# Normalizing and splitting images in the second stage, half an image per unit

## The chip, the cores and the metric

One core of a Trainium2 chip runs the whole program. Its engines work side by side and meet at semaphores: TensorE (PE) multiplies matrices, VectorE (DVE), ScalarE (ACT) and GpSimd (POOL) do elementwise work, SyncE (SP) issues the DMAs. The time is the device time of one execution in microseconds (us); the median of several runs counts.

## The reference, cut to what matters

The input x has 16 images of 32 channels and 128 x 128 pixels, in f32.

```python
x = x + conv_a(gn(x))     # per-image 3x3 depthwise weights mixed by an attention, then a 1x1 conv
x = x + conv_b(gn(x))
# gn: each channel of each image minus its mean, over its standard deviation
# conv_b: hidden = 1x1 conv 32 -> 192, then a 3x3 depthwise conv; q, k, v = split(hidden)
#         out = irfft2(rfft2(8x8 patches of q) * rfft2(8x8 patches of k))
#         result = w_out @ (v * layernorm_over_channels(out))
```

## The kernel before, in words

**First stage.** The loop over images b from -1 to 15 convolves image b on TensorE (`conv_step`, L530), while image b+1 is centred on ScalarE and image b+2 is loaded and its statistics taken on VectorE. ScalarE evacuates the result x2 (`evacuate`, L731), VectorE takes its statistics (`second_stats`), and from them `shifts` makes scale2 and shift2, the second normalization of that image. SyncE stores x2 to DRAM (`store_x2`). Then the image is normalized in place (`norm`, L746, ScalarE), its f16 value is written to xh (`high`, L757, ScalarE), and what f16 leaves over to xl (`low`, L968, VectorE). `store_xn` (L335) writes both, padded to rows of 130, to the DRAM tensor xn_d, in 8 DMAs of 260 KB.

**Second stage.** There are 32 units u, half an image each; b = u // 2. The buffer xs of a unit holds 66 rows of 130 columns, high and low parts on four groups of 32 partitions. There are three such buffers. For each unit VectorE copies eight windows out of xs (`window`, L1109, r from 0 to 7), TensorE multiplies them into 32 groups (`hidden_group`, L575), and ScalarE copies these out (L817). That is the front of a unit; TensorE interleaves it with the end of the unit before (the "tail"): its v chunks (`v_chunk`, L590, which read xs as well), turns (L603) and projections (L612). Then comes the spectral part: for each of eight octets m TensorE makes q (L650) and k (L662), ScalarE copies q (L859), VectorE multiplies (L1215) and adds (`spectrum`, L1201, L1203), and after octets 2, 4 and 7 come the four inverse transforms (L683), copied out to Y by ScalarE (L872). VectorE then normalizes Y over channels, gates it with v (L1144) and adds the projected result to the residual (`residual`, L1151), which was loaded from x2 in DRAM and is stored to `out`.

**The order of the DMAs.** All are issued by SyncE, in the order of its program, and a wait holds back everything behind it. In the second stage one turn of its loop, for u from 1 on, is before the change:

```python
if u < LAST:
    sp.wait_ge(s_hidden_mm, 32 * u + 1)
    load_xs(u + 1)                # L348: 4 loads of 536 KB, each waited for
store_res(u - 1)                  # L404: waits for the last residual; 4 stores, each waited for
sp.wait_ge(s_inverse_mm, 4 * u + 3)
load_res(u, 0)                    # L395: 2 loads of 256 KB
sp.wait_ge(s_res_in, 64 * u + 32)
load_res(u, 1)                    # 2 more, not waited for
```

The functions that the change touches, and their callers:

Of the kernel before, what the change touches and what calls it, by code (L numbers as in the profile page):

```python
# [24 lines left out]
X_SCALE = 256.0  # L25
# [43 lines left out]
def build(nc, t, out):  # L69
# [4 lines left out]
    NB, C, H, W = x.shape  # L74
# [9 lines left out]
    SUMS = 6  # L84

# [7 lines left out]
    with ctx:  # L93
# [19 lines left out]
        s_xs_in = [semaphore(f"xs_in{s}") for s in range(3)]  # L113
        s_res_in = semaphore("res_in")
        s_out_stored = semaphore("out_stored")
# [4 lines left out]
        s_win_room = semaphore("win_room")  # L120
# [57 lines left out]
        s_xl_ready = semaphore("xl_ready")  # L178

# [55 lines left out]
        def take_tables(name):  # L235
# [13 lines left out]
        tiny = {n: take(c) for n, c in (("v_scale", 1), ("v_shift", 1), ("pixel_stats", 96), ("var_eps", 32), ("rstd", 32))}  # L249
# [22 lines left out]
            ("x2_bias0", 1), ("x2_bias1", 1), ("shift1", 1), ("scale2", 1), ("shift2", 1),  # L272
# [20 lines left out]
        win = [take(1632, f16) for _ in range(3)]  # L293
# [21 lines left out]
        def _(sp):  # L315
# [47 lines left out]
            for b in range(-1, NB + 2):  # L363
# [43 lines left out]

            sp.wait_ge(s_xn_out, 128 * NB)
            load_res(0, 0)
            load_res(0, 1)  # L410
# [14 lines left out]
        def _(pool):  # L425
# [11 lines left out]
            for s in range(3):  # L437
                pool.memset(win[s][:, 16 * WIN:1632].bitcast(f32), 0.0).then_inc(s_win_room, 1)
            pool.wait_ge(s_pool_consts, 2)
            pool.wait_ge(s_pads_zero, 2)  # L440
            pool.wait_ge(s_win_room, 3)
# [25 lines left out]
        def _(pe):  # L467
# [111 lines left out]
            def v_chunk(u, k, jr, groups, between):  # L579
# [6 lines left out]
                for tap in range(9):  # L586
                    dy, dx = tap // 3, tap % 3
                    for s in range(2):
                        row = 8 * (2 * s + jr) + dy
                        mm = pe.matmul(v_banks[chunk % 3][64 * s:64 * s + 64, :], v_w[:, 64 * tap:64 * tap + 64],  # L590
                                       at(xs[u % 3], row * WP + 32 * k + dx, [32 * WP, 2], [WP, 8], [1, 32]),
# [123 lines left out]
        def _(act):  # L715
# [10 lines left out]
            def evacuate(b, k):  # L726
                if k == 0 and b > 2:
                    act.wait_ge(s_xl_ready, 4 * (b - 2))
# [11 lines left out]
            def norm(b, i):  # L740

                if b is not None:
# [3 lines left out]
                    act.activation(piece, piece, ACT.Identity, bias=tiny["shift2"], scale=tiny["scale2"]).then_inc(s_x2n_ready, 1)  # L746
# [533 lines left out]
```

## Time and profile before

| | |
|---|---|
| median of 3 runs | 2265.87 us (2260.75 to 2266.81) |
| the profiled execution | 2273.27 us, its span 2271.2 us |
| TensorE busy | 2145.7 us, 94% |
| VectorE busy | 1741.6 us, 77% |
| ScalarE busy | 1432.6 us, 63% |
| GpSimd busy | 517.1 us, 23% |
| mean granted clock of TensorE | 0.971 of full speed |
| DMA moved | 248.21 MB, 109 GB/s over the span |

Busy time is the time in which an engine executes an instruction; an engine can also be idle because it waits for another, or for a DMA. The granted clock is the share of full speed (2.4 GHz) that the chip lets TensorE have. The profile also shows the convolutions ending at 501 us and the first v chunk of the second stage at 560 us; from there on the units repeat.

### The profile page before, as it was taken

How to read it: one execution, taken by the hardware profiler on the slowest of the kernel's cores; microseconds unless marked ns; L12 is line 12 of the kernel's file. 1: busy time of each engine (PE TensorE's matmuls, PEld its weight loads, DVE VectorE, ACT ScalarE, POOL GpSimd, SP SyncE). 2: the span in 40 equal slices, each digit the busy share in tenths (PEclk: the TensorE clock that was granted, in tenths of full speed). 3: DMA queues.
4: the chain of work that ended last, by engine and by line, in shares of the span. 5: the costliest groups of instructions: out<-in, count | busy, mean ns of one | idle time of the engine just before them, and what ended most of it. 6: DMA issues, size and time to landing. Idle time of an engine off the chain costs nothing.

```text
span 2271.2 us, 101012 instructions
## 1 busy us (share of the span) xinstructions
PE 2145.7 (94%) x45303; PEld 1364.8 (60%) x45303; DVE 1741.6 (77%) x4186; ACT 1432.6 (63%) x2629; POOL 517.1 (23%) x323
## 2 busy tenths in 40 slices
PE   6888888977999999999999999999999999999997
PEld 3333333336666666666666666666666666666664
DVE  4666666645888888888888888788888888878886
ACT  3456655656666666666666666666666666666662
POOL 1000000000332222322222222233322322322222
PEclk9989988888999999999999999999999999999998
DMA  7688888876333333333333333333433333333312
GB/s 144 163 220 224 223 219 219 207 193 157 79 83 84 79 90 86 79 78 79 79 79 81 85 83 79 83 88 79 97 85 82 88 79 88 79 78 79 79 40 57
DMA packets 60386, 248.21 MB, mean 109 GB/s; under 512 B 12393, under 2 KB 12658, under 8 KB 53810
## 3 DMA queue, kind: packets, MB, share of 16 engines
q1 hardware_dynamic: 59954, 241.75, 44.9%
q8 instruction: 357, 5.85, 1.1%
q14 instruction: 75, 0.61, 0.1%
HBM read 139.99 MB, written 101.72 MB: 106 GB/s over the span
## 4 chain that ended last, share of the span: by engine, by line
PE 90%; issue 4%; ACT 2%; DVE 2%; DMA 1%; POOL 0%; SPq 0%; POOLq 0%; ACTq 0%
PE bank L590 24%; PE bank L530 17%; PE bank L575 10%; PE bank L662 10%; PE bank L650 9%; PE bank L603 7%; PE bank L683 6%; PE bank L612 5%; DVE arena L1215 2%; ACT arena L826 1%; ACT arena L731 1%; DMA arena<-tap_rows_in 1%; PE bank L544 0%; ACT arena L817 0%; PE bank L492 0%
## 5 line engine op out<-in xcount | busy, mean ns | idle before, releaser
L459 POOL TENSOR_TENSOR arena<-arena 128x8 f32<-128x8 f32 x256 | 492.8, 1925 | 1238.0 <-DVE arena L1125 1235.5
L590 PE MATMUL bank<-arena 128*64 128x512 f16 x4608 | 690.2, 394 | 0.0
L817 ACT ACTIVATE arena<-bank 100x512 f32<-100x512 f32 x1024 | 581.8, 599 | 110.1 <-PE bank L575 79.4
L575 PEld LDWEIGHTS bank<-arena 128*64 128x64 f16 (+1 forms) x8192 | 328.7, 104 | 232.6 <-issue 22.3
L530 PE MATMUL bank<-arena 32*32 32x508 f32 (+1 forms) x9216 | 384.2, 655 | 51.1 <-issue 36.4
L575 PE MATMUL bank<-arena 128*64 128x128 f16 (+1 forms) x8192 | 389.3, 220 | 18.0 <-DVE arena L1109 11.5
L1215 DVE TENSOR_TENSOR arena<-bank,arena 128x512 f32<-128x512 f32 x512 | 328.9, 684 | 48.2 <-issue 44.9
L826 ACT ACTIVATE arena<-bank,arena 128x256 f32<-128x256 f32 x512 | 261.3, 561 | 114.1 <-PE bank L603 111.2
L859 ACT ACTIVATE arena<-bank 128x512 f32<-128x512 f32 x256 | 152.9, 597 | 225.7 <-PE bank L650 223.9
L1144 DVE TENSOR_TENSOR arena<-arena,bank 128x512 f32<-128x512 f32 x256 | 174.8, 683 | 139.6 <-ACT arena L826 139.6
L650 PE MATMUL bank<-arena 100*32 100x128 f32 x8192 | 276.1, 275 | 1.3 <-ACT arena L817 1.3
L662 PE MATMUL bank<-arena 100*32 100x128 f32 x8192 | 274.8, 274 | 0.2 <-issue 0.2
L1119 DVE BATCH_NORM_STATS2 arena<-arena 128x6 f32<-128x128 f32 x1024 | 221.6, 278 | 65.4 <-ACT arena L872 65.4
L590 PEld LDWEIGHTS bank<-arena 128*64 128x64 f16 x4608 | 206.6, 109 | 95.8 <-issue 11.9
L530 PEld LDWEIGHTS bank<-arena 32*32 32x32 f32 x9216 | 144.7, 107 | 189.6 <-issue 157.6
L872 ACT ACTIVATE arena<-bank 128x256 f32<-128x256 f32 x512 | 155.1, 389 | 147.5 <-PE bank L683 147.5
L662 PEld LDWEIGHTS bank<-arena 100*32 100x32 f32 x8192 | 222.3, 110 | 29.2 <-DVE arena L1215 23.5
L650 PEld LDWEIGHTS bank<-arena 100*32 100x32 f32 x8192 | 217.4, 110 | 19.7 <-ACT arena L817 1.6
L1139 DVE TENSOR_TENSOR arena<-arena 128x512 f32<-128x512 f32 x256 | 177.3, 692 | 37.3 <-POOL arena L459 17.3
L603 PEld LDWEIGHTS bank<-arena 128*128 128x128 f32 x1024 | 133.9, 195 | 107.5 <-issue 68.8
L603 PE MATMUL bank<-arena 128*128 128x128 f32 x1024 | 181.6, 300 | 8.2 <-ACT arena L826 7.1
L683 PE MATMUL bank<-arena 32*64 32x256 f32 x5120 | 171.6, 384 | 15.3 <-DVE arena L1215 12.9
(113 smaller groups left out, 1655.9 us busy)
## 6 DMA issues: line engine op xcount, KB each, us to landing
arena<-xn_d SPq DMA_DIRECT2D x128, 536.2 KB, 4.8
xn_d<-arena SPq DMA_DIRECT2D x130, 260.0 KB, 4.4
x_d<-arena SPq DMA_DIRECT2D x64, 512.0 KB, 8.1
arena<-x_d SPq DMA_DIRECT2D x128, 256.0 KB, 4.1
out<-arena SPq DMA_DIRECT2D x128, 256.0 KB, 2.7
arena<-x_in SPq DMA_DIRECT2D x32, 544.0 KB, 9.6
arena<-x_in SPq DMA_DIRECT2D x32, 528.0 KB, 9.4
arena<-spectra_in SPq DMA_DIRECT2D x1, 384.0 KB
```

The lines of the kernel that those rows point to most:

```text
L459: pool.tensor_tensor(tiny["rstd"][:, slot], tiny["var_eps"][:, slot], powers, ALU.pow).then_inc(s_root, 1)
L530: mm = pe.matmul(at(psum_of(t, r)[32 * c:32 * c + 32, :], low, [W, 4], [1, high - low]), conv_w[b % 2][32 * r:32 * r + 32, 32 * tap:32 * t ...
L575: mm = pe.matmul(ring[g % len(ring)][low:high, 128 * i:128 * i + 128], w[:, first + low:first + high], hidden_w, start=True, stop=True)
L590: mm = pe.matmul(v_banks[chunk % 3][64 * s:64 * s + 64, :], v_w[:, 64 * tap:64 * tap + 64], at(xs[u % 3], row * WP + 32 * k + dx, [32 * WP ...
L603: tr = pe.transpose(t_bank[:, 128 * i:128 * i + 128], at(Y, 8 * k + 4 * jr + i, [32, 128]), ident)
L650: mm = pe.matmul(q_bank[32 * c:32 * c + 32, first:first + 128], G_q[0:WIN, 64 * ch + 32 * part:64 * ch + 32 * part + 32], hwin[0:WIN, 128 ...
L662: mm = pe.matmul(k_banks[m % 2][32 * c:32 * c + 32, first:first + 128], G_k[0:WIN, 64 * ch + 32 * part:64 * ch + 32 * part + 32], hwin[0:W ...
L683: mm = pe.matmul(i_banks(e)[c][64 * lam:64 * lam + 64, 256 * (e % 2):256 * (e % 2) + 256], small["inverse"][32 * c:32 * c + 32, 64 * table ...
L817: act.activation(h_rows[0:WIN, :, first:first + 4], ring[g % len(ring)][0:WIN, :].rearrange("p (i c) -> p c i", i=4), ACT.Copy).then_inc(s ...
L826: ins = act.activation(at(gated[jr], 256 * lam, [32, 8], [8, 4], [1, 8]), at(banks[4], 64 * lam, [8, 8], [128, 4], [1, 8]), ACT.Identity, ...
L1119: ins = dve.bn_stats(T["pixel_stats"][:, first:first + 6], at(Y, 2048 * s + 4 * p + j, [32, 64], [1, 2]))
L1215: dve.tensor_tensor(prod[:, first:first + 512].rearrange("p (a b x) -> p a b x", a=2, b=2), at(k_banks[m % 2], 256 * quad, [128, 2], [0, 2 ...
```

## The change

Only images 0 and 1 (`EARLY = 2`) are still normalized, split and stored to xn_d in the first stage. For the other 14 images the first stage keeps scale2 and shift2 (now one column for each image) and does no `norm`, `high`, `low` or `store_xn`. The second stage does this work instead, in 28 halves: in each of the units 0 to 27, SyncE loads 64 raw rows of x2 (`load_half`), ScalarE does `norm_half` twice and `high_half` twice between the q copies of the spectral part, VectorE `low_half` once after octet 4 and once at the end, and SyncE stores the result with 8 DMAs (`store_half`). The half made in unit u is unit u + 4. Its buffers take the place of the third xs buffer. With two buffers left, the upper 42 rows of the next xs (`load_top`, one DMA at a time) are loaded once the last v chunk of the unit before has been made, and the lower 24 rows (`load_bottom`, two at a time) in the next turn. `load_res` is now called one turn later for the unit that ended, and waits for both of its pairs. The windows of a unit wait for the upper rows at r = 0 and for the lower ones at r = 5.

```diff
+    EARLY = 2
+    TOP = 42
+    HALVES = 2 * (NB - EARLY)
...
-        xs_late = take(HALF * WP, f16)
+        half_x2 = take(2048)
         top[0] = max(top[0], stage1_end)
-        xs = [take(HALF * WP, f16) for _ in range(2)] + [xs_late]
+        xs = [take(HALF * WP, f16) for _ in range(2)]
+        half_high, half_low = [take(16 * WP, f16) for _ in range(2)]
...
-            def load_xs(u, paced=True):
-                b, half = divmod(u, 2)
+            def load_xs(u, landed, first, last, at_once):
+                b, h = divmod(u, 2)
                 for g in range(4):
-                    src = xn_d[b, g % 2, :, half * (H // 2):half * (H // 2) + HALF, :].rearrange("c h w -> c (h w)")
-                    sp.dma_start(xs[u % 3][32 * g:32 * g + 32, :], src).then_inc(s_xs_in[u % 3], 16)
-                    if paced:
-                        sp.wait_ge(s_xs_in[u % 3], 64 * (u // 3) + 16 * (g + 1))
+                    src = xn_d[b, g % 2, :, h * (H // 2) + first:h * (H // 2) + last, :].rearrange("c h w -> c (h w)")
+                    sp.dma_start(xs[u % 2][32 * g:32 * g + 32, first * WP:last * WP], src).then_inc(landed[u % 2], 16)
+                    if (g + 1) % at_once == 0:
+                        sp.wait_ge(landed[u % 2], 64 * (u // 2) + 16 * (g + 1))
+            def load_top(u, at_once):
+                load_xs(u, s_top_in, 0, TOP, at_once)
+            def load_bottom(u, at_once):
+                load_xs(u, s_bottom_in, TOP, HALF, at_once)
...
-                if b == NB + 1:
-                    load_xs(1, paced=False)
-                if older is not None:
+                if older is not None and older < EARLY:
                     sp.wait_ge(s_xl_ready, 4 * (older + 1))
                     store_xn(older)
-                if b == NB - 3:
-                    sp.wait_ge(s_xn_out, 128 * (older + 1))
+                if b in (NB - 3, NB + 1):
+                    u = (b - NB + 3) // 4
+                    sp.wait_ge(s_xn_out, 128)
                     sp.wait_ge(s_pads_stored, 32)
-                    load_xs(0, paced=False)
+                    load_top(u, 8)
+                    load_bottom(u, 8)
...
-            def load_res(u, pair):
-                for s in range(2):
-                    p0 = 64 * pair + 32 * s
-                    sp.dma_start(res[p0:p0 + 32, :].rearrange("p (l r) -> p l r", l=2),
+            def load_res(u):
+                for part in range(4):
+                    pair, s = divmod(part, 2)
+                    sp.dma_start(res[32 * part:32 * part + 32, :].rearrange("p (l r) -> p l r", l=2),
                                  image_rows(x2_d, u // 2, u % 2, pair, s)).then_inc(s_res_in, 16)
+                    if s == 1:
+                        sp.wait_ge(s_res_in, 64 * u + 16 * (part + 1))
...
+            def load_half(u):
+                b, h = divmod(u + 2 * EARLY, 2)
+                if u > 0:
+                    sp.wait_ge(s_half_low, 2 * u)
+                for g in range(4):
+                    first = (64 * h + 16 * g) * W
+                    sp.dma_start(half_x2[32 * g:32 * g + 32, :], x2_d[b, :, first:first + 16 * W]).then_inc(s_half_in, 16)
+                    if g in (1, 3):
+                        sp.wait_ge(s_half_in, 64 * u + 16 * (g + 1))
+            def store_half(u):
+                b, h = divmod(u + 2 * EARLY, 2)
+                done = 128 * EARLY + 128 * u
+                if u == 0:
+                    sp.wait_ge(s_half_pads, 2)
+                sp.wait_ge(s_half_low, 2 * (u + 1))
+                for part, buf in ((0, half_high), (1, half_low)):
+                    for g in range(4):
+                        first = 1 + 64 * h + 16 * g
+                        sp.dma_start(xn_d[b, part, :, first:first + 16, :].rearrange("c h w -> c (h w)"),
+                                     buf[32 * g:32 * g + 32, :]).then_inc(s_xn_out, 16)
+                        if g == 3:
+                            sp.wait_ge(s_xn_out, done + 64 * (part + 1))
+            for s in range(3):
+                sp.wait_ge(s_x2_out[s], 64 * len(range(s, NB, 3)))
+            sp.wait_ge(s_shift2, NB)
+            load_half(0)
             for u in range(1, LAST + 1):
+                sp.wait_ge(s_inverse_mm, 4 * u - 1)
+                if u > 1:
+                    load_bottom(u, 2)
+                load_res(u - 1)
+                if u <= HALVES:
+                    store_half(u - 1)
+                if u < HALVES:
+                    load_half(u)
                 if u < LAST:
-                    sp.wait_ge(s_hidden_mm, 32 * u + 1)
-                    load_xs(u + 1)
+                    sp.wait_ge(s_v_mm, 8 * u)
+                    sp.wait_ge(s_xn_out, 128 * EARLY + 128 * min(u, HALVES))
+                    load_top(u + 1, 1)
                 store_res(u - 1)
-                sp.wait_ge(s_inverse_mm, 4 * u + 3)
-                load_res(u, 0)
-                sp.wait_ge(s_res_in, 64 * u + 32)
-                load_res(u, 1)
+            sp.wait_ge(s_inverse_mm, 4 * LAST + 4)
+            load_res(LAST)
             store_res(LAST)
...
             def norm(b, i):
-                if b is not None:
+                if b is not None and b < EARLY:
                     act.wait_ge(s_shift2, b + 1)
                     act.wait_ge(s_x2_out[b % 3], 64 * (b // 3 + 1))
                     piece = x2[b % 3][:, QPIX // 2 * i:QPIX // 2 * (i + 1)]
-                    act.activation(piece, piece, ACT.Identity, bias=tiny["shift2"], scale=tiny["scale2"]).then_inc(s_x2n_ready, 1)
+                    act.activation(piece, piece, ACT.Identity, bias=tiny["shift2"][:, b:b + 1], scale=tiny["scale2"][:, b:b + 1]).then_inc(s_x2n_ready, 1)
...
+            def norm_half(u, i):
+                if u < HALVES:
+                    b, piece = u // 2 + EARLY, half_x2[:, 1024 * i:1024 * i + 1024]
+                    act.wait_ge(s_shift2, b + 1)
+                    act.wait_ge(s_half_in, 64 * (u + 1))
+                    act.activation(piece, piece, ACT.Identity, bias=tiny["shift2"][:, b:b + 1], scale=tiny["scale2"][:, b:b + 1]).then_inc(
+                        s_half_norm, 1)
+            def high_half(u, i):
+                if u < HALVES:
+                    act.wait_ge(s_half_norm, 2 * u + i + 1)
+                    act.wait_ge(s_xn_out, 128 * EARLY + 128 * u)
+                    act.activation(half_high.rearrange("p (h w) -> p h w", w=WP)[:, 8 * i:8 * i + 8, 1:W + 1],
+                                   half_x2[:, 1024 * i:1024 * i + 1024].rearrange("p (h w) -> p h w", w=W), ACT.Copy).then_inc(s_half_high, 1)
             def spectral(u, tail):
                 for m in range(8):
...
                     act.activation(q_sb[m % 2], q_bank, ACT.Copy).then_inc(s_q_copied, 1)
                     if m == 0 and tail is not None:
                         turned_out(tail, 3, 1)
+                    if m in (1, 4):
+                        norm_half(u, m // 4)
+                    if m in (2, 6):
+                        high_half(u, m // 4)
...
-                    dve.wait_ge(s_xs_in[u % 3], 64 * (u // 3 + 1))
+                    dve.wait_ge(s_top_in[u % 2], 64 * (u // 2 + 1))
+                if r == TOP // 8:
+                    dve.wait_ge(s_bottom_in[u % 2], 64 * (u // 2 + 1))
                 dve.tensor_copy(win[(8 * u + r) % 3][:, 0:16 * WIN].rearrange("p (j y x) -> p j y x", y=10, x=10),
-                                     at(xs[u % 3], 8 * r * WP, [8, 16], [WP, 10], [1, 10])).then_inc(s_win_ready, 1)
+                                     at(xs[u % 2], 8 * r * WP, [8, 16], [WP, 10], [1, 10])).then_inc(s_win_ready, 1)
...
+            def low_half(u, i):
+                if u < HALVES:
+                    dve.wait_ge(s_half_high, 2 * u + i + 1)
+                    padded = lambda a: a.rearrange("p (h w) -> p h w", w=WP)[:, 8 * i:8 * i + 8, 1:W + 1]
+                    dve.tensor_tensor(padded(half_low), half_x2[:, 1024 * i:1024 * i + 1024].rearrange("p (h w) -> p h w", w=W),
+                                      padded(half_high), ALU.subtract).then_inc(s_half_low, 1)
...
+                    if n == 9:
+                        low_half(u, 0)
                 if u < LAST:
                     for r in range(3):
                         window(u + 1, r)
-            dve.wait_ge(s_win_room, 3)
+                low_half(u, 1)
```

## Rows read from the trace of the kernel before

**Rows 1.** Stretches: length, busy PE, PEld, DVE, ACT, POOL; clock; DMA share; GB/s.

```profile
64.46:121.06 56.60, 50.21 (x1177) 21.24 (x1178) 35.07 (x100) 31.07 (x37) 2.19 (x6) 0.91 0.76 192
149.36:478.51 329.15, 286.97 (x6469) 119.55 (x6470) 212.53 (x557) 190.64 (x210) 12.03 (x33) 0.89 0.85 217
478.51:501.10 22.59, 21.57 (x580) 10.31 (x580) 10.77 (x20) 11.69 (x11) 0.70 (x1) 1.00 0.79 190
501.10:534.80 33.70, 14.37 (x264) 11.82 (x263) 14.84 (x26) 27.89 (x42) 0.70 (x1) 0.66 0.81 192
...
613.77:667.49 53.72, 53.11 (x1122) 36.73 (x1124) 44.28 (x104) 35.82 (x72) 15.43 (x8) 1.00 0.36 83
```

**Rows 2.** Waits of PE, 700 to 2188: us in total, times, longest.

```profile
PE bank L683 <- DVE arena L1215: 11.7, 27, 0.8
```

**Rows 3.** Waits of SyncE's queue, 700 to 2188: us in total, times, longest.

```profile
SPq L348 <- DMA arena<-xn_d: 407.3, 81, 7.0
SPq L404 <- DMA out<-arena: 227.0, 84, 4.1
SPq L395 <- DMA arena<-x_d: 106.6, 28, 4.6
```

**Rows 4.** Timeline of SyncE, 1400 to 1462: start, from first issue to last, line.

```profile
1422.82 5.67 SPq L395 DMA_DIRECT2D arena<-x_d  x4
```

**Rows 5.** DMA issues, 700 to 2188: count, size of each, median us to landing.

```profile
arena<-xn_d SPq DMA_DIRECT2D x108, 536.2 KB, 4.8
out<-arena SPq DMA_DIRECT2D x112, 256.0 KB, 2.7
arena<-x_d SPq DMA_DIRECT2D x112, 256.0 KB, 4.1
```

**Rows 6.** DMA issues in the first stage, 120 to 420.

```profile
xn_d<-arena SPq DMA_DIRECT2D x80, 260.0 KB, 4.4
```

**Rows 7.** Timeline of PE, 1400 to 1462: start, us, line.

```profile
1416.99 1.12 PE L683 MATMUL bank<-arena 32*64 32x256 f32 x32
...
1450.41 1.02 PE L612 MATMUL bank<-arena 128*64 128x512 f32 x4
```

**Rows 8.** Timeline of DVE, 1400 to 1462; in brackets the idle time before.

```profile
1413.64 1.29 DVE L1215 TENSOR_TENSOR arena<-bank,arena 128x512 f32<-128x512 f32 x2 [0.53 <-issue]
...
1417.19 1.29 DVE L1215 TENSOR_TENSOR arena<-bank,arena 128x512 f32<-128x512 f32 x2 [0.20 <-issue]
1418.39 1.54 DVE L1109 COPY arena<-arena 128x1600 f16<-128x1600 f16 x3
...
1433.81 0.57 DVE L1109 COPY arena<-arena 128x1600 f16<-128x1600 f16 x1
...
1440.51 0.68 DVE L1151 TENSOR_TENSOR arena<-bank,arena 128x512 f32<-128x512 f32 x1
```

**Rows 9.** Timeline of ACT, 1400 to 1462.

```profile
1455.92 0.60 ACT L859 ACTIVATE arena<-bank 128x512 f32<-128x512 f32 x1 [0.89 <-PE bank L650]
1457.71 0.60 ACT L859 ACTIVATE arena<-bank 128x512 f32<-128x512 f32 x1 [1.20 <-PE bank L650]
```

**Rows 10.** Groups of instructions by shape, 120 to 420: busy, mean ns, idle before.

```profile
L968 DVE TENSOR_TENSOR arena<-arena 128x1024 f16<-128x1024 f32 x40 | 48.8, 1222 | 0.3
...
L738 ACT ACTIVATE arena<-arena 128x1024 f32<-128x1024 f32 x20 | 22.9, 1147 | 0.0
```

**Rows 11.** The chain that ended last, 495 to 562: start, us, what.

```profile
503.60 1.81 ACT arena L757
...
555.20 2.38 issue
```

**Rows 12.** The page's costliest groups, window copies of ScalarE.

```profile
L817 ACT ACTIVATE arena<-bank 100x512 f32<-100x512 f32 x1024 | 581.8, 599 | 110.1 <-PE bank L575 79.4
```

**Rows 13.** Busy time by stretch around a stall of PE.

```profile
154.00:156.00 2.00, 0.00 (x0) 0.00 (x0) 0.83 (x1) 0.55 (x1) 0.00 (x0) 1.00 0.69 240
158.00:170.00 12.00, 12.00 (x183) 3.81 (x151) 3.71 (x13) 2.29 (x2) 0.89 (x2) 0.50 0.71 169
```

More of the change, by code:

```diff
@@ L112, in build @@
         s_transforms_in = semaphore("transforms_in")
-        s_xs_in = [semaphore(f"xs_in{s}") for s in range(3)]
+        s_top_in = [semaphore(f"top_in{s}") for s in range(2)]
+        s_bottom_in = [semaphore(f"bottom_in{s}") for s in range(2)]
         s_res_in = semaphore("res_in")
+        s_half_in = semaphore("half_in")
         s_out_stored = semaphore("out_stored")
@@ L248, in build @@
         powers = take(8)
-        tiny = {n: take(c) for n, c in (("v_scale", 1), ("v_shift", 1), ("pixel_stats", 96), ("var_eps", 32), ("rstd", 32))}
+        tiny = {n: take(c) for n, c in (("v_scale", 1), ("v_shift", 1), ("pixel_stats", 96), ("var_eps", 32), ("rstd", 32), ("scale2", NB), ("shift2", NB))}
         phases = top[0]
@@ L287, in build @@
         res = take(2048)
-        xs_late = take(HALF * WP, f16)
+        half_x2 = take(2048)
         top[0] = max(top[0], stage1_end)
-        xs = [take(HALF * WP, f16) for _ in range(2)] + [xs_late]
+        xs = [take(HALF * WP, f16) for _ in range(2)]
+        half_high, half_low = [take(16 * WP, f16) for _ in range(2)]
         G_q = take(64 * 64)
         G_k = take(64 * 64)
-        win = [take(1632, f16) for _ in range(3)]
+        win = [take(16 * WIN, f16) for _ in range(3)]
         block = ctx.enter_context(nc.Block())
@@ L436, in _ @@
             pool.memset(xl.bitcast(f32), 0.0).then_inc(s_pads_zero, 1)
-            for s in range(3):
-                pool.memset(win[s][:, 16 * WIN:1632].bitcast(f32), 0.0).then_inc(s_win_room, 1)
+            for buf in (half_high, half_low):
+                pool.memset(buf.bitcast(f32), 0.0).then_inc(s_half_pads, 1)
             pool.wait_ge(s_pool_consts, 2)
             pool.wait_ge(s_pads_zero, 2)
-            pool.wait_ge(s_win_room, 3)
+            pool.wait_ge(s_half_pads, 2)
             for b in range(-1, NB + 1):
@@ L590, in v_chunk @@
                         mm = pe.matmul(v_banks[chunk % 3][64 * s:64 * s + 64, :], v_w[:, 64 * tap:64 * tap + 64],
[L591 removed]
+                                       at(xs[u % 2], row * WP + 32 * k + dx, [32 * WP, 2], [WP, 8], [1, 32]),
                                        start=tap == 0, stop=tap == 8)
@@ L745, in norm @@
                     piece = x2[b % 3][:, QPIX // 2 * i:QPIX // 2 * (i + 1)]
-                    act.activation(piece, piece, ACT.Identity, bias=tiny["shift2"], scale=tiny["scale2"]).then_inc(s_x2n_ready, 1)
+                    act.activation(piece, piece, ACT.Identity, bias=tiny["shift2"][:, b:b + 1], scale=tiny["scale2"][:, b:b + 1]).then_inc(s_x2n_ready, 1)
             def high(b, i):
-                if b is not None:
+                if b is not None and b < EARLY:
                     rows = slice(16 * i, 16 * i + 16)
@@ L803, in _ @@
                         evacuate(here, k)
-            high(NB - 2, 0)
-            high(NB - 2, 1)
             h_rows = hwin.rearrange("p (c j) -> p c j", j=128)
@@ L838, in front @@
                 if tail is None:
-                    some(16)
-                    norm(NB - 1, 0)
-                    norm(NB - 1, 1)
-                    some(8)
-                    high(NB - 1, 0)
-                    some(8)
-                    high(NB - 1, 1)
-                    act.wait_ge(s_xl_ready, 4 * (NB - 1))
+                    for s in (1, 2):
+                        act.wait_ge(s_x2_out[s], 64 * len(range(s, NB, 3)))
+                    act.wait_ge(s_st[2], NCH * (NB - 1))
+                    some(32)
                     return
@@ L868, in inverse_out @@
                 if u == 0 and e == 0:
-                    act.wait_ge(s_xl_ready, 4 * NB)
+                    act.wait_ge(s_x2_out[0], 64 * len(range(0, NB, 3)))
+                    act.wait_ge(s_st[2], NCH * NB)
                 act.wait_ge(s_inverse_mm, 4 * u + e + 1)
@@ L962, in low @@
             def low(b, i):
-                if b is not None:
+                if b is not None and b < EARLY:
                     dve.wait_ge(s_xh_ready, 2 * b + 1 + i // 2)
@@ L1095, in _ @@
                 first_stats(later, range(3, NCH))
-            for i in range(4):
-                low(NB - 2, i)
             Y4 = Y.rearrange("p (s c j) -> p s c j", s=2, j=32)
@@ L1167, in front @@
                     windows(4)
-                    for i in range(4):
-                        low(NB - 1, i)
                     return
```

21 lines of the change are left out of this document (12 added, 9 removed).

## The prediction, made before the changed kernel was run

> **What bounds the kernel now.** I read the busy time by stretch first [rows 1]. From 64 to 501 us the images are convolved one by one; the last, with no input load left to run, takes 22.59 us at a granted clock of 1.00, the eleven before it 329.15 / 11 = 29.92 us at 0.89, with the DMA engines 85% busy. From 560 us on each of the 32 units (half an image) takes 53.72 us, of which TensorE is busy 53.11: the second stage is TensorE's, and nothing it waits for there exceeds 11.7 us over 28 units [rows 2]. VectorE (44.28) and ScalarE (35.82) have room. The view that matters for this change is a third one, SyncE's queue: the DMAs are issued in one order, and the queue stands still at every wait. Its waits for landings [rows 3], its own timeline [rows 4] and the landing times [rows 5] give the price of one round (issue, land, wait).
>
> **The queue's loop today.** Single loads of xn (536 KB) land after 4.8 us, so four paced ones cost about 20; a store of `out` (256 KB) waits 227.0/84 = 2.7 us and is 0.3 in issue, 3.0 a round, 12.1 for four. A pair of residual loads (2 x 256 KB) waits 106.6/28 = 3.81; the timeline has four issues and that wait in 5.67 us, so an issue is 0.46 and a pair round 0.92 + 3.81 = 4.73. The second pair is not waited for today. Sum 12.1 + 5.7 + about 20 = 38 us of 53.72: SyncE has some 15 us to spare in each unit.
>
> **The queue's loop after.** Each iteration u from 1 to 28 holds, every group waited for:
> - lower rows of xs: 2 pairs of 195 KB. Nearest rows: a single 2.7 store plus an issue (3.2) and the 4.73 pair. I take 4.0, as 390 KB lies closer to 512: 8.0.
> - residual: 2 pairs of 256 KB, now both waited for: 9.5.
> - store of the split half: 2 groups of 4 x 130 KB. Nearest: 2.7 plus three issues (4.1), and the first stage's xn stores, 4.4 plus three issues (5.8) [rows 6]. 520 KB is the size that lands in 4.8 alone; I take 4.9: 9.8.
> - load of the next raw half: 2 pairs of 256 KB: 9.5.
> - upper 42 rows of the next xs, one at a time: 4 x 341 KB, between 2.7 (256 KB) and 4.8 (536 KB); on the line between them 3.3, and since loads here (4.73 a pair) cost more than stores I take 3.6: 14.4.
> - `out`: 12.1.
>
> Sum 63.3 us; with all the low ends 56.4, with all the high ends 71.4. Even the low sum exceeds 53.72. From iteration 2 on nothing in the queue can hide behind TensorE, because everything is serial in one queue: the loop becomes the period of the second stage.
>
> **What is late, and when.** Marks of a unit, counted from its first window copy at 1418.39: last v chunk finished at +32.0 (the projection behind it starts at 1450.41 [rows 7]); window 5, the first that needs the lower rows, at +15.4; first residual at +22.1 [rows 8]; ScalarE free for norm_half after the second q copy at +38.1 [rows 9]; the next unit's first window at +53.7. The inverse that starts iteration u ends at -0.3. Count from that point of unit 0. Iteration 1 (no lower rows): residual 9.5, store 19.3, load 28.8, wait for the v chunk until 32.3, top landed 46.7, the first window of unit 2 due at 54.0: covered. `out` ends at 58.8. Iteration 2: lower rows 66.8, residual 76.3, store 86.1, raw half 95.6 (ScalarE wanted it at 92.2), so the window of unit 3 slips from 107.8 to 95.6 + 16.0 = 111.6. From then each of iterations 3 to 27 adds 63.3: 111.6 + 25 x 63.3 = 1694.1. Iteration 28 loads no raw half; it still has waits of 3.1 us for the lower rows and 2.8 us for the residual, then 53.7: 1753.7. Without delay that window would be due at 0.3 + 28 x 53.72 = 1504.5. So the loss is 249 us, and 26 us for each us of the loop. In the steady state TensorE idles in three places of a unit: before window 5, before the first residual, and before norm_half in ScalarE, which holds the q copies. Iterations 29 to 31 have neither store nor raw half (44 us) and run at 53.7.
>
> **New compute.** Two norm_half (128x1024; the same form takes 1.147 us [rows 10]) and two high_half go between q copies where ScalarE idles 0.89 to 1.20 us [rows 9]: nothing. low_half (1.222 us [rows 10]) stands after the spectrum of octet 4, where VectorE has 0.53 us idle and 0.20 more before octet 7 [rows 8]: 0.5 us late for the last inverse. In a unit that waits for the queue it is hidden; if the queue were covered it would cost 28 x 0.5 = 14 us. The pools' pads and the four extra columns: nothing.
>
> **First stage.** Fourteen images lose 8 stores, two norms, two highs and four lows. The two images convolved before any xn store took 56.60 / 2 = 28.30 us, the eleven whose stores now vanish 29.92 [rows 1]: 1.62 x 11 = 17.8 us. Bounds: 0, and 81 if they came to 22.59. I stay at the low end, since the stalls of TensorE and the clock falls after them are there in the 28.30 too (0.91). Removing ScalarE and VectorE work there gives nothing more, neither is full.
>
> **Unit 0.** From 501.1 to 534.8 normalizing and splitting the last two images stands between the window copies; the chain goes from the last evacuation straight into high at 503.6 [rows 11]. Without that work there follow at once 32 window copies of 0.599 us [rows 12], 19.2: 2.5 + 19.2 = 21.7 instead of 33.7, and the gap of 2.38 us at 555.2 goes: 14.4 us.
>
> **Sum.** 2271.2 span + 2.1 around it = 2273.3 profiled; - 17.8 - 14.4 + 248.5 = 2489.6. The profiled execution is 7.4 us above the median of 2265.87, so 2482.
>
> **A rule against the row.** [Rows 5] show 4.8 us for 536 KB and 2.7 for 256. The Trainium skill, "DMA: Bandwidth & Descriptors", section "Anatomy of one DMA — SWDGE (gpsimd) path", gives 2.0 us fixed plus bytes at 436 GB/s for another issuing path; that fits the 2.7 but makes 3.3 of the 4.8. By it, an estimate with the issues above added, the loop would be about 51 us and the change a gain. The row speaks against it for the larger loads.
>
> **Rivals.** (a) Transfers hardly grow with size and the loop is covered: each single or first landing at 2.7 gives top 10.8, lower rows 6.3, store 8.2, and a raw half whose contiguous rows land like a store 6.3, with 9.5 and 12.1: 53.2, below 53.72. Then 2273.3 - 32.2 + 14 - 7.4 = 2248, faster. It decides at a loop of about 55.3, where the loss equals the 32 won. For it: 2.7 for 256 KB; against it: every load row. Chance 0.07; that the loss just cancels the gain, 0.02. (b) The loop is the bound but cheap, 55.5 to 59: 2275 to 2370. Chance 0.1. (c) The forecast, 59 to 68.5: 2370 to 2620. Chance 0.69. (d) TensorE's clock falls in each of the three waits. After a stall of 3.98 us (154 to 158) the clock stood at 0.50 for 12 us [rows 13], 6 us lost. Three such are 18, and 54.2 + 18 = 72 exceeds the loop's 63.3: 26 x 9 = 234 more, about 2715. It decides from 9 us lost per unit. Against it: a later unit with less wait has less to fall for, and the wait itself absorbs the slow time. Chance 0.12. The Trainium skill, "TensorE: Matmul & The Clock Gate", section "HAM oscillation — how this bites in real kernels", describes a loop whose DMA waits bring the clock down in every turn; that speaks for (d).
>
> **How the numbers follow.** Time 2482; range 2360 to 2650, which leaves out (a), most of (d) and the edge of (b). Within 0.3% (6.8 us, what this kernel's measurement can tell from no change): 0.02. Faster 0.07, slower 0.91.
>
> **What would show it.** SyncE's queue after should have no long wait on VectorE or TensorE from iteration 3 to 27, and a period near 63 us; TensorE idle near 10 us a unit ending on the raw half, the lower rows and the residual; windows of images near 28 us in the first stage; unit 0 some 14 us shorter. If the period of a unit is 54 us and SyncE still waits for the last residual, the round prices are wrong and (a) holds; if SyncE waits for the last v chunk, TensorE's clock is the cause.

## The result, and the profile after

The changed kernel takes 2413.83 us (median; 2410.51 to 2425.2), the kernel before 2266.34 beside it: a ratio of 1.0644, 95% interval 1.0612 to 1.0675. It is 6.4% slower. Forecast were 2482 and a range of 2360 to 2650. The profiled execution took 2415.88 us, its span is 2414.0.

The page of the kernel after: busy time, granted clock in 40 slices, and the shares of the chain that ended last.

```profile
PE 2197.0 (91%) x45303; PEld 1378.7 (57%) x45303; DVE 1743.2 (72%) x4186; ACT 1442.0 (60%) x2685; POOL 516.0 (21%) x322
...
PEclk9998999989999999999999999999999999999999
...
DMA 64%; PE 26%; SPq 5%; issue 3%; ACT 1%; DVE 0%; POOL 0%; ACTq 0%; DVEq 0%; POOLq 0%
DMA arena<-xn_d 25%; DMA arena<-x_d 20%; PE bank L582 15%; DMA out<-arena 13%; DMA xn_d<-arena 5%; PE bank L642 3%; SPq L447 3%; PE bank L714 1%; SPq L358 1%; PE bank L702 1%; PE bank L655 1%; PE bank L627 1%; PE bank L664 1%; PE bank L735 1%; SPq L411 1%
```

TensorE is still busy 91% of the time, yet it holds only 26% of the chain; DMAs hold 64%. Busy share and bound have parted. The timeline of SyncE in the kernel after shows one whole turn of its loop and the start of the next (start, time from the first issue to the last, line; L358 are loads of xs, L422 stores of `out`, L411 the residual, L447 the half store, L433 the raw half):

```profile
1462.55 11.00 SPq L358 DMA_DIRECT2D arena<-xn_d  x4
1476.82 9.52 SPq L422 DMA_DIRECT2D out<-arena  x4
1488.67 4.50 SPq L358 DMA_DIRECT2D arena<-xn_d  x4
1496.27 5.55 SPq L411 DMA_DIRECT2D arena<-x_d  x4
1505.75 5.51 SPq L447 DMA_DIRECT2D xn_d<-arena  x8
1513.13 5.38 SPq L433 DMA_DIRECT2D arena<-x_d  x4
1522.21 7.46 SPq L358 DMA_DIRECT2D arena<-xn_d  x3
```

From one start to the next lie 14.27 us (upper rows), 11.85 (`out`), 7.60 (lower rows), 9.48 (residual), 7.38 (half store) and 9.08 (raw half): 59.66 us, with no gap between them. Over 27 turns, from the lower rows at 588.18 to those at 2208.14, the mean is 60.0 us, against the 53.72 of [rows 1]. SyncE's waits in the kernel after, 700 to 2300 us (in total, times, longest), show what it waits for:

```profile
SPq L358 <- DMA arena<-xn_d: 349.2, 106, 4.4
SPq L422 <- DMA out<-arena: 206.9, 80, 3.9
...
SPq L467 <- PE bank L642: 32.7, 3, 15.1
SPq L419 <- DVE arena L1220: 1.6, 2, 0.8
```

All but five of its waits are for landings. For TensorE it waits three times in 1600 us, at the end of the window, where the turns have no raw half to load, and for the last residual hardly at all. In turn the other engines wait for the DMAs; VectorE and ScalarE in the kernel after, 700 to 2300, each a view of its own:

```profile
DVE arena L1220 <- DMA arena<-x_d: 100.4, 26, 4.8
DVE arena L1178 <- DMA arena<-xn_d: 41.5, 22, 5.3
```

```profile
ACT arena L907 <- DMA arena<-x_d: 16.9, 13, 2.4
```

These are the three places named in the prediction: first residual, window 5, raw half. The busy time by stretch of the kernel after (columns as in [rows 1]):

```profile
149.37:459.55 310.18, 273.13 (x6468) 115.55 (x6469) 162.97 (x513) 107.59 (x166) 11.97 (x33) 0.94 0.62 155
459.55:481.98 22.43, 21.18 (x588) 10.77 (x588) 8.19 (x20) 5.25 (x10) 0.70 (x1) 1.00 0.43 98
481.98:531.25 49.27, 36.92 (x926) 29.24 (x928) 24.01 (x50) 29.54 (x59) 0.69 (x1) 0.86 0.50 118
...
588.18:2208.14 1619.96, 1499.33 (x30242) 1010.08 (x30240) 1255.51 (x2861) 1074.65 (x2049) 412.67 (x217) 0.97 0.44 109
```

Eleven images take 310.18 us where they took 329.15 [rows 1]. The first v chunk of the second stage starts at 531.25 instead of 560.00. From there to the end of the span it is 1882.8 us instead of 1711.2: 28.8 us are won before it, 171.5 lost behind it.

How far one profile of the images can be trusted is seen from the experiments below. Eight of them (e1 to e6, e8, e10) leave the first stage as it is in the changed kernel, and in their profiles the eleven images take 309.5 to 321.1 us. The 310.18 lies near the short end, so of the 19.0 us that these two profiles show as won, a part is luck; against the slowest of the nine it would be 8.

### The profile page after: what moved, and what is told of

Read it like the earlier page. It is cut to its first block, busy times and chain, and to the rows that moved or that the text cites. A ratio compares the mean times of both kernels' runs of the same rounds, so it can differ in the third digit from the quotient of the medians.

```text
span 2414.0 us, 101600 instructions
## 1 busy us (share of the span) xinstructions
PE 2197.0 (91%) x45303; PEld 1378.7 (57%) x45303; DVE 1743.2 (72%) x4186; ACT 1442.0 (60%) x2685; POOL 516.0 (21%) x322
## 4 chain that ended last, share of the span: by engine, by line
DMA 64%; PE 26%; SPq 5%; issue 3%; ACT 1%; DVE 0%; POOL 0%; ACTq 0%; DVEq 0%; POOLq 0%
DMA arena<-xn_d 25%; DMA arena<-x_d 20%; PE bank L582 15%; DMA out<-arena 13%; DMA xn_d<-arena 5%; PE bank L642 3%; SPq L447 3%; PE bank L714 1%; SPq L358 1%; PE bank L702 1%; PE bank L655 1%; PE bank L627 1%; PE bank L664 1%; PE bank L735 1%; SPq L411 1%
## 5 line engine op out<-in xcount | busy, mean ns | idle before, releaser
L642 PE MATMUL bank<-arena 128*64 128x512 f16 x4608 | 698.7, 398 | 0.0
L582 PE MATMUL bank<-arena 32*32 32x508 f32 (+1 forms) x9216 | 370.9, 632 | 45.4 <-issue 30.4
L702 PE MATMUL bank<-arena 100*32 100x128 f32 x8192 | 281.2, 277 | 21.1 <-ACT arena L923 18.6
L714 PE MATMUL bank<-arena 100*32 100x128 f32 x8192 | 277.3, 275 | 1.2 <-issue 1.0
L664 PE MATMUL bank<-arena 128*64 128x512 f32 x512 | 171.9, 673 | 84.6 <-DVE arena L1220 84.4
L655 PE MATMUL bank<-arena 128*128 128x128 f32 x1024 | 188.2, 308 | 9.3 <-ACT arena L877 7.1
```

What stands on the lines that cost most here:

```text
L582: mm = pe.matmul(at(psum_of(t, r)[32 * c:32 * c + 32, :], low, [W, 4], [1, high - low]), conv_w[b % 2][32 * r:32 * r + 32, 32 * tap:32 * t ...
L655: tr = pe.transpose(t_bank[:, 128 * i:128 * i + 128], at(Y, 8 * k + 4 * jr + i, [32, 128]), ident)
L664: mm = pe.matmul(f_bank[64 * jr:64 * jr + 64, :], small["w_out"], gated[jr], start=True, stop=True)
L702: mm = pe.matmul(q_bank[32 * c:32 * c + 32, first:first + 128], G_q[0:WIN, 64 * ch + 32 * part:64 * ch + 32 * part + 32], hwin[0:WIN, 128 ...
L714: mm = pe.matmul(k_banks[m % 2][32 * c:32 * c + 32, first:first + 128], G_k[0:WIN, 64 * ch + 32 * part:64 * ch + 32 * part + 32], hwin[0:W ...
```

## The experiments

Medians of one batch stand beside the kernel before in the same batch: 2268.12 for the first four, 2267.02 for the next four, 2264.94 for the last four. All start from the changed kernel and its 2413.83 unless another is named.

**e2, the upper rows in pairs.**

```diff
-                    load_top(u + 1, 1)
+                    load_top(u + 1, 2)
```

> The changed kernel with the upper rows of xs loaded two at a time instead of one at a time, nothing else. Theory (the period is the sum of the rounds): four rounds of 3.6 us become two of about 5.3, the loop loses 3.7 us of 60, so 27 x 3.7 = 100 us less: about 2314 us. If the stalls of TensorE and its clock set the period and not the sum, the time moves by less than 30 us.

Measured: 2308.93 us, ratio to before 1.0187 (1.0156 to 1.0218). 105 us less where 100 were expected. The period of the second stage follows the sum of the rounds: between the first stores of `out` of one unit and the next it is 55.8 us on average over 26 turns, in the changed kernel 59.95.

**e3, one group left out.**

```diff
-                if u < HALVES:
-                    load_half(u)
...
-                    act.wait_ge(s_half_in, 64 * (u + 1))
...
+                    act.wait_ge(s_half_in, 64)
+                    if u > 0:
+                        act.wait_ge(s_half_low, 2 * u)
+                        act.activation(piece, piece, ACT.Copy).then_inc(s_half_norm, 1)
```

> The changed kernel without the raw-half loads of units 1 to 27 (norm_half then copies the stale half in place of scaling it, so the images from the third on are not computed rightly); all compute instructions and all other DMAs stay. Theory: the loop loses its 9.1 us and is 51 us, below TensorE's 53.7, so the whole loss of the second stage goes but for some us: about 2255 us. If the new work on ScalarE and VectorE were part of the loss it would stay in this kernel: 14 us or more above that.

Measured: 2264.73 us, ratio 1.0011 (0.9989 to 1.0032). 149 us less with as many elementwise instructions as before (from u = 1 on `norm_half` copies instead of scaling). It is 10 us above what was expected, less than the 14 that were named for the elementwise work. SyncE waits for TensorE again in nearly every turn; waits of SyncE in this kernel, 700 to 2200 (L465 stands before the upper rows):

```profile
SPq L465 <- PE bank L640: 147.5, 27, 14.0
```

**e4, only the elementwise work left out,** and with it SyncE's two waits for its results.

```diff
-                if u > 0:
-                    sp.wait_ge(s_half_low, 2 * u)
...
-                sp.wait_ge(s_half_low, 2 * (u + 1))
...
-                    if m in (1, 4):
-                        norm_half(u, m // 4)
-                    if m in (2, 6):
-                        high_half(u, m // 4)
...
-                    if n == 9:
-                        low_half(u, 0)
...
-                low_half(u, 1)
```

> The changed kernel without norm_half, high_half and low_half (the images from the third on are then not computed), with all DMAs kept. Theory: the new work hides in waits for SyncE's queue, so the time stays within 15 us of 2414; a little less is possible because the store no longer waits for low_half. Rival (the new elementwise work delays TensorE by 0.5 us or more in each unit): 14 us or more less.

Measured: 2397.82 us, ratio 1.0572 (1.0536 to 1.0609). 16 us less, just outside the 15 allowed and also at the foot of the rival's 14. Since e3 keeps this work and recovers 149, it is at most a tenth of the loss. The trace places the 16 us in the second stage: the first v chunk starts at 530.3 us, about where it did, and the 26 turns between the first stores of `out` of units 1 and 27 take 59.37 us each instead of 59.95, 15 us in all. SyncE's loop is still the bound there. Whether its turn is shorter for want of the work or of the two waits, this run does not tell.

**e9, fewer halves.**

```diff
-    EARLY = 2
+    EARLY = 8
```

> The changed kernel with EARLY = 8 in place of 2: six more images are normalized and split in the first stage, 16 halves in place of 28 are made in the second. If each turn of SyncE's loop that holds a half costs 60 - 53.7 = 6.3 us, 12 turns less give 76 us back and the six images cost 1.7 us each: 2414 - 76 + 10 = 2348 us. If the loss came from the two xs buffers and not from the halves, it would stay above 2400.

Measured: 2341.28 us, ratio 1.0332 (1.0309 to 1.0356). 73 us less, 66 expected. The loss comes with the halves, not with having two xs buffers.

**e1, no pacing anywhere.** All waits inside the groups go; of store_res the last stays, since the next residual overwrites its buffer.

```diff
-                    if s == 1:
-                        sp.wait_ge(s_res_in, 64 * u + 16 * (part + 1))
...
-                    if g in (1, 3):
-                        sp.wait_ge(s_half_in, 64 * u + 16 * (g + 1))
...
-                        if g == 3:
-                            sp.wait_ge(s_xn_out, done + 64 * (part + 1))
...
-                    load_bottom(u, 2)
+                    load_bottom(u, 8)
...
-                    load_top(u + 1, 1)
+                    load_top(u + 1, 8)
```

> The changed kernel with every wait for a landing inside a group of SyncE's DMAs taken out, that is the waits that only pace it: lower and upper rows of xs, residual, raw half and half stores are issued without a wait between them, and of the four waits in the store of out only the last is kept. Same bytes, same computation, same buffers. Theory (the queue's sum of serial rounds is the period): the loop falls from 60 us to some 25 to 35 us, below TensorE's 53.7, SyncE waits again for TensorE or VectorE, a unit takes 54 to 54.5 us, and the whole about 2250 us (2414 less 27 x 6). Rival 1 (the bytes, not the waits, cost the time: 6.3 MB a unit contend in the DMA engines): above 2330. Rival 2 (the new work on ScalarE and VectorE or the two buffers cost the time): above 2380.

Measured: 2335.01 us, ratio 1.0306 (1.0265 to 1.0346). The theory failed in its number by 85 us, and the number is what rival 1 had named for bytes that contend (above 2330); this run alone could not refute it. The first half of the theory held. Of SyncE's waits in this kernel, 700 to 2200, all but the last row are for TensorE and VectorE, so its loop has room and bounds nothing:

```profile
SPq L358 <- PE bank L636: 469.6, 26, 27.4
SPq L420 <- DVE arena L1214: 299.6, 26, 14.0
SPq L451 <- PE bank L729: 223.3, 27, 9.9
SPq L461 <- DMA xn_d<-arena: 91.3, 25, 5.0
```

But TensorE now has waits that it had not, 700 to 2200:

```profile
PE bank L708 <- issue: 21.8, 16, 2.8
PE bank L696 <- issue: 19.7, 18, 2.7
```

"issue" is time in which it waits for no semaphore that the profile shows. One of them in its timeline, and the stretches around it:

```profile
1481.19 0.38 PE L708 MATMUL bank<-arena 100*32 100x128 f32 x3
1484.32 1.71 PE L708 MATMUL bank<-arena 100*32 100x128 f32 x27 [2.75 <-issue]
```

```profile
1478.00:1482.00 4.00, 3.57 (x127) 3.19 (x116) 3.32 (x7) 3.04 (x6) 0.00 (x0) 1.00 0.76 162
1482.00:1484.30 2.30, 0.00 (x0) 0.00 (x0) 1.59 (x4) 0.98 (x2) 0.00 (x0) 1.00 0.00 0
1484.30:1488.00 3.70, 3.68 (x63) 3.32 (x64) 1.61 (x3) 0.06 (x1) 0.00 (x0) 0.54 0.02 4
```

The four upper-row loads were issued together at 1474.11 and kept the DMA engines busy until about 1481; the stall follows, and the clock is at 0.54 after it. So the loss that the pacing caused was replaced by one that the pacing had kept away. A new theory: a burst (several DMAs issued with no wait between them) hurts beside the spectral part, where TensorE issues 32 matmuls in 0.9 us, and not in the front, where its v chunks take 0.4 us each. The next two kernels split the bursts by place.

**e5, bursts in the front only.** Lower rows, residual, half store and raw half unpaced; upper rows and `out` as in the changed kernel.

> The changed kernel with only the groups that SyncE issues in the front part of a unit left unpaced: lower rows of xs, residual, half stores, raw half. The upper rows (one at a time) and the four stores of out (each waited for), which run in the spectral part, stay as they are. Theory A (bursts in the spectral part make TensorE stall and lower its clock, bursts in the front part do not; SyncE's loop is now covered): no stalls of TensorE on issue beyond those of before, units of 54 to 54.5 us, 2250 to 2265 us. Theory B (a burst costs TensorE wherever it is): above 2290. If the loop of SyncE is still over 53.7 us, it is seen in its timeline.

Measured: 2258.12 us, ratio 0.9961 (0.9946 to 0.9977). Stalls of TensorE on issue, 700 to 2200, are 4.0 us in all, the largest this:

```profile
PE bank L708 <- issue: 2.8, 5, 1.0
```

And the burst itself, 20 DMAs in the front, by stretch:

```profile
1454.80:1466.00 11.20, 11.20 (x186) 7.54 (x184) 9.64 (x30) 9.80 (x20) 7.98 (x4) 1.00 0.92 232
1466.00:1472.00 6.00, 6.00 (x86) 3.46 (x82) 4.59 (x15) 4.79 (x10) 1.84 (x2) 1.00 0.93 234
```

17 us with the DMA engines at 0.92, and TensorE busy without a gap at full clock. Removing the serial waits of the front alone gives back 156 us. The queue's loop is the cause of the loss. Rival 1 of e1, bytes that contend, falls too: e5 moves the same bytes and is 77 us faster than e1.

**e6, bursts in the spectral part only.** The opposite choice: upper rows and `out` unpaced, the front paced.

> The other half: the front groups paced as in the changed kernel, the upper rows and the stores of out issued at once. Sum of SyncE's rounds: 33.6 in the front, some 7 and 5 for the bursts, 46 us, covered. Theory A: the stalls of the wholly unpaced kernel are all here, so its time again, about 2335. Theory B: some of both, about 2290.

Measured: 2373.91 us, ratio 1.0453 (1.0406 to 1.0499). Theory A had 2335, so the size missed by 39; its sign is clear, 116 us above e5. Waits of TensorE, 700 to 2200:

```profile
PE bank L714 <- issue: 28.7, 18, 3.6
PE bank L702 <- issue: 24.1, 13, 4.2
```

With only two of the six groups in bursts, all its stalls on issue come to 63 us (e1: 44), and the clock over this stretch is 0.97, in e1 0.99 and in e5 1.00. SyncE again waits for VectorE (252 us) and TensorE (298 us), so it is not its loop. That puts the difference to e1 into more stalls and their slow clock; why the same bursts make more of them is not settled.

**What TensorE waits for in these stalls.** The page of every run has a DMA queue of the kind instruction. In the changed kernel it reads:

```profile
q8 instruction: 357, 5.85, 1.1%
```

357 packets of 16 KB beside 90,606 matmuls and weight loads of TensorE: one for each 254. In the stall of e1 shown above, the queues from 1469 to 1481.7 us have data packets alone (first row), and the next instruction packet comes at 1481.78, in the stretch from 1481.7 to 1483 (second row):

```profile
q1 hardware_dynamic: 188, 1.40, 49.5%
```

```profile
q8 instruction: 1, 0.02, 5.7%
```

It is over at 1482.96, and TensorE goes on at 1484.32. All 18 stalls of e1 that are longer than 1 us (700 to 2200) end so, 1.2 to 1.5 us after such a packet. Before these 18 packets TensorE had started 404 to 540 matmuls and weight loads since the packet before; the median over all 234 packets is 232.5, and the most that went without such a stall is 435. In the changed kernel the most is 404, in e5 425, and neither has a stall above 1 us. By these numbers TensorE runs out of instructions when a packet of them comes too late. In e5 the packets are late too, in time (1454.25, then 1465.33, in the middle of its burst), but TensorE started only 352 matmuls and weight loads between them. What holds the packet back, the burst's data in the same DMA engines by its timing, is argued and not shown.

**e7, the stores' traffic put back into the first stage.** Eight DMAs an image to a scratch tensor, for images 2 to 13.

```diff
+                if older is not None and EARLY <= older < 14:
+                    sp.wait_ge(s_quarter_xn, min(b + 2, NB))
+                    store_xn(older, scratch_d, s_scratch)
```

> The changed kernel with the xn stores of images 2 to 13 put back into the first stage, but to a scratch tensor and from the same buffers, whose contents no longer change; no normalizing or splitting comes back. If the traffic of the stores is what lengthened an image, the eleven images from the fifth on go back from 28.2 to 29.9 us and the time rises by about 18 us. If it was the work of ScalarE and VectorE, they stay at 28.2 and the time at 2414.

The eleven images, by stretch:

```profile
150.24:479.49 329.25, 285.52 (x6468) 116.67 (x6469) 162.30 (x511) 107.37 (x166) 11.98 (x33) 0.91 0.82 217
```

329.25 us, as in [rows 1], though ScalarE is busy 107 us there instead of 191. It also lies above all nine profiles without this traffic (309.5 to 321.1). The traffic lengthens an image, not the elementwise work. The whole took 2419.33 us, ratio 1.0659 (1.0626 to 1.0693), 5.5 more than the changed kernel and not 18; the ranges of the two overlap (2410.55 to 2429.72), so the total alone would not have decided. Between the two profiled executions the difference is 14 us.

**e8, low_half late** (e5 with one line moved).

```diff
-                    if n == 9:
-                        low_half(u, 0)
+                low_half(u, 0)          # after the last product, before the window copies
```

> Front groups unpaced as in the kernel beside it, and the first low_half moved from behind octet 4 to behind the last product, before the window copies. The wait of the last inverse for VectorE should fall back from 0.57 to 0.42 us or less, 4 us in all; if the rest of the 0.6 us by which a unit exceeds that of before in the covered kernels hangs on it, 15 us.

Measured: 2254.59 us, ratio 0.9949 (0.9931 to 0.9968); 3.5 us below e5, the small expectation; the ranges of the two overlap, so this difference alone shows little. In the two profiles TensorE's wait for the last product falls from 15.2 to 11.2 us over 27 units, and the 26 turns from one unit's first store of `out` to the next take 53.99 us each instead of 54.26. The three kernels below (e10 to e12), which keep the move, have 53.9 to 54.0.

**e10, unit 0 late** (e8, and in unit 0 norm_half after octets 4 and 5, high_half after 6 and 7).

> Front groups unpaced, low_half late, and in unit 0 alone norm_half after octets 4 and 5 and high_half after 6 and 7, because its raw half lands only after octet 2. The wait of ScalarE for that landing (6 us) goes: 5 us less than the kernel without it, about 2250 us. If the landing is then waited for at the later place, nothing.

Measured: 2246.80 us, ratio 0.9925 (0.9900 to 0.9951). It is the fastest of all and beats both kernels, the one before by less than 1%. The first v chunk starts at 527.81 us, in e8 at 536.43, in e5 at 531.25, but the images vary by as much between these profiles. Counted from the start of the last matmul of the convolutions it comes after 43.6 us, in e8 after 47.8 and in e5 after 47.9, and ScalarE no longer waits before `norm_half` in unit 0.

**e11 and e12, pacing the first stage** (e10, with waits after pairs, or after groups, of input loads and x2 stores).

```diff
+                if b > 1:
+                    sp.wait_ge(s_x_in[b % 3], 64 * (b // 3) + 16 * (quarters[-1] + 1))
...
+                    if c in (1, 3):         # e12: if c == 3
+                        sp.wait_ge(s_x2_out[b % 3], 64 * (b // 3) + 16 * (c + 1))
```

> The kernel beside it, with the DMAs of the first stage paced: SyncE waits after each pair of input loads and after each pair of x2 stores. If bursts make TensorE stall there too, the stalls on issue (30 us from 64 to 455 us) and the clock of 0.94 go: up to 5.8 us an image, 80 us in all. The rounds are four pairs of 1 MB an image, some 7 us each, 28 us, which is the present length of an image: then nothing is won, since the queue becomes the bound, and the stalls alone go. I expect between -30 and +20 us.

> The same with a wait only after each group (two loads, four stores, two loads), so at most 2 MB in flight. Less pacing: stalls fall in part, the queue has room. I expect -40 to +5 us against the kernel with no pacing in the first stage.

Measured: e11 2360.83 us, ratio 1.0428 (1.0406 to 1.0449); e12 2326.20, ratio 1.0260 (1.0240 to 1.0281). 114 and 79 us above e10: both expectations missed on the bad side. The chain of e11 between 200 and 270 us shows why:

```profile
212.49 6.61 DMA arena<-x_in
...
219.72 6.84 DMA x_d<-arena
...
227.17 6.14 DMA x_d<-arena
...
233.69 7.46 DMA arena<-x_in
```

The four pairs are the chain, and behind the last one stand the statistics and the next convolution; an image takes 36.8 us (stores start at 219.12 and 255.92), not the 28 that the sum of rounds gave. Stalls on issue from 64 to 455 us did fall, from 30.8 us in e10 to 16.3 in e11 (2.2 and 1.5 us an image), so pacing has fewer stalls here too, at a price that this stage cannot pay.

## Why the prediction was right, point by point

**The cause and the sign: right, shown.** The prediction said that six groups, each waited for in one queue, take the place of TensorE as the bound. e2, e3 and e5 each shorten the queue's turn in another way, e9 has fewer turns with a half, and they get 105, 149, 156 and 73 us back. Rival (a), a loop that is covered, is refuted by SyncE's waits; (b) by the period of 60.0.

**The terms of the turn.** Upper rows 14.4 forecast, 14.3 measured; `out` 12.1, 11.85; residual 9.5, 9.48; raw half 9.5, 9.1; lower rows 8.0, 7.6. The half store was mis-sized: 9.8 forecast, 7.38 measured. The landing of the kernel after, 700 to 2300 us:

```profile
arena<-x_d SPq DMA_DIRECT2D x204, 256.0 KB, 3.9
arena<-xn_d SPq DMA_DIRECT2D x106, 341.2 KB, 3.6
out<-arena SPq DMA_DIRECT2D x106, 256.0 KB, 2.6
xn_d<-arena SPq DMA_DIRECT2D x200, 130.0 KB, 2.2
arena<-xn_d SPq DMA_DIRECT2D x108, 195.0 KB, 3.2
```

Four stores of 130 KB land 2.2 us after their issue, each, while I priced them as one load of 520 KB. By the row of the 256 KB store (2.7) and the issues, the low end of 4.1 a group was the nearer one. The turn came to 60.0 in place of 63.3, and that is most of what the forecast is off: 26 x 3.3 = 86 us less loss, 163 in place of 249; measured are 171.5. With unit 0 and the images (below), and a profiled execution 2.1 us above the median where 7.4 were taken off, the forecast comes to the 2414 measured. Small slips in the sum change nothing: the steps add to 249.2, not 248.5, and from norm_half to the next window it is 15.6 us, not 16.0.

Here the Trainium skill, "DMA: Bandwidth & Descriptors", section "Anatomy of one DMA — SWDGE (gpsimd) path", gave by the estimate in the prediction a loop of some 51 us, and so a gain. By its formula 341 KB take 2.8 us, and the row has 3.6. The measurement decides against using it for this queue.

**What is late, and when: right.** All three waits are there. The residual takes the largest share (100 us over 26 turns), lower rows 42, the raw half 17. TensorE itself idles less than the 10 us a unit that the prediction gave, as the next point shows.

**Rival (d), the clock: there, but at no cost.** The clock of the second stage fell from 1.00 to 0.97, and TensorE was busy 1499.33 / 27 = 55.5 us a turn instead of 53.1. Its waits over 700 to 2200 us come to 114 us in 25 turns, 4.6 a turn; 55.5 + 4.6 is the 60. The slow time fits into waits that were there anyway, as the prediction argued. It would have counted from 9 us a turn, and was 2.4. From 700 to 2200 us the granted clock fell to its lower level 21 times in 25 turns, each time for less than 7 us. This agrees with the Trainium skill, "TensorE: Matmul & The Clock Gate", section "HAM oscillation — how this bites in real kernels", on when the clock falls, in nearly every turn of a loop with DMA waits, but here it cost nothing.

**New compute: the size met by luck.** Forecast were 0.5 us a unit if the queue is covered, 14 us. e5, covered, needs 1724.7 us from its first v chunk to the end of its span, before 1711.2: 13.5 more. e8, with low_half late, 1715.7. The total fits, its parts do not. Over the same 26 turns, counted from first v chunk to first v chunk, the kernel before takes 1397.9 us and e5 1410.5. Of the 12.6 us more, the wait for the last product, which was to be all of it, is 4.2 (0.16 us a unit, not 0.5); stalls on issue are 4.0, and TensorE is busy 4.1 longer. The step that was mis-sized is that low_half makes the last inverse 0.5 us late. e8, with low_half late, takes 1403.6: the wait for the last product is back at the 10.8 us of before. What makes TensorE busy longer is not tested.

**First stage and unit 0.** Images: 17.8 forecast, 329.15 - 310.18 = 19.0 between the two profiles, and e7 shows the traffic as the cause, which the prediction had taken from two images alone. That the sizes meet so closely is luck, since the nine profiles with this first stage give 8 to 20 us. Unit 0: 14.4 forecast, 9.6 measured (501.10 to 560.00 before, 481.98 to 531.25 after). What failed is that no new wait was counted there. ScalarE's timeline in the kernel after:

```profile
511.95 1.24 ACT L907 ACTIVATE arena<-arena 128x1024 f32<-128x1024 f32 x1 [6.01 <-DMA arena<-x_d]
```

and the chain that leads to it:

```profile
496.88 10.48 DMA arena<-x_d
507.71 4.15 DMA arena<-x_d
```

The first raw half is queued behind the last x2 stores and the eight loads of xs for unit 1, lands at 511.9, and norm_half holds the q copies behind it. The same mechanism as in the loop, overlooked at its start.

## What to carry to other kernels

Work that moves under an idle engine also moves its DMAs into a queue; add up that queue's turn, issue by issue and landing by landing, and hold it against the compute of the turn. When the sum is too large, take out waits where TensorE issues slowly and keep the transfers paced where it issues fast: here the same change then gives 0.4% (e5) instead of costing 6.4%, and 0.75% with low_half and unit 0's norm_half moved as well (e10). A wait that only paces can be worth more than the time that it seems to waste, and it can also cost more: in the first stage the same pacing made 79 to 114 us of loss.

## What the runs showed of the hardware that was not expected

- Four loads of 341 KB issued together landed 5.4 us after issue (median, e1) where one at a time took 3.6 each. They made TensorE stall on issue for up to 2.8 us in e1 and, with four stores, up to 4.2 us in e6, at the end of the burst or just behind it in those looked at, with the clock at 0.50 to 0.57 behind it.
- Twenty DMAs at once, 17 us with the DMA engines at 0.92, made no stall at all beside the front of a unit (e5). What differs is how fast TensorE issues: 186 matmuls in 11.2 us there, 32 in 0.9 us in the spectral part.
- The stalls end 1.2 to 1.5 us after a late packet of TensorE's instructions (all 18 of e1 above 1 us). The Trainium skill, "Runtime: NRT & Kernel Launch", section "Instruction fetch mechanics", describes such a fetch by DMA and calls its cost mostly hidden. The traces agree on the fetch. They agree on its cost in the changed kernel and in e5, with 1.4 and 4.0 us of stalls on issue, and not in e1 and e6, with 44 and 63 us.
